# A pre-norm decoder layer: keys scaled earlier on ScalarE, scores scaled in four pieces, one residual and two transposes moved

## What is computed

```python
x = x + mixer(layernorm(x))            # in-projection, conv of 4 taps, silu, ssd, silu(z) gate, rms norm, W_out
q = rmsnorm(layernorm(x) @ Wq + bq) * qn_w
k = rmsnorm(ctx @ Wk + bk) * kn_w      # "k-hat": keys times 1/rms, per head
v = ctx @ Wv + bv
scores = q @ k.T / sqrt(128) + mask    # 1/rms of q is applied to the scores
x = x + softmax(scores) @ v @ Wo
h = silu(bit_linear(layernorm(x), w_gate)) * bit_linear(layernorm(x), w_up)
x = x + bit_linear(rms_norm(h, ln_weight), w_down)
```

## Time and profile before

| | us |
|---|---|
| median of 3 executions | 1190.26 (1189.74 to 1191.51) |
| profiled execution, device time | 1191.23 |
| its span, first to last instruction | 1189.5 |

### The profile page before, as it was taken

How to read it: one execution, slowest core, us unless ns; L and a number is a source line. 1 busy time by engine, 2 the same in 40 slices (tenths; PEclk the granted TensorE clock), 3 DMA queues, 4 the chain that set the end, 5 groups by cost and what they waited for, 6 DMA issues and landing times.

```text
span 1189.5 us, 34826 instructions
## 1 busy us (share of the span) xinstructions
PE 1119.2 (94%) x11405; PEld 983.7 (83%) x11405; DVE 1005.5 (85%) x2509; ACT 819.7 (69%) x2066; POOL 935.8 (79%) x1514
## 2 busy tenths in 40 slices
PE   4889999999999999999999999999999999999964
PEld 3678888898888889888888988888898888888753
DVE  4766898898889889888988988898898889888666
ACT  4586777677667767766776776677677667766641
POOL 4788788888888888888888888888888888878651
PEclk8899999999999999999999999999999999999987
DMA  8311101111110111111011111101111110121000
GB/s 297 87 50 24 33 17 31 37 37 35 33 37 15 29 37 37 35 33 37 15 29 37 37 35 33 37 15 29 37 37 35 33 37 15 29 35 30 22 9 23
DMA packets 103306, 46.31 MB, mean 39 GB/s; under 512 B 80352, under 2 KB 101600, under 8 KB 103008
## 3 DMA queue, kind: packets, MB, share of 16 engines
q1 hardware_dynamic: 100336, 45.75, 14.8%
q10 hardware_dynamic: 2928, 0.03, 0.1%
HBM read 23.93 MB, written 4.19 MB: 24 GB/s over the span
## 4 chain that ended last, share of the span: by engine, by line
PE 66%; DVE 13%; ACT 13%; issue 4%; POOL 2%; DMA 1%; ACTq 1%; POOLq 0%; DVEq 0%; SPq 0%
PE bank L1800 18%; PE bank L1882 5%; PE bank L1860 5%; PE bank L1718 4%; PE bank L1690 4%; PE bank L1691 4%; PE bank L1692 4%; DVE hh L1389 3%; DVE hh L1382 3%; ACT kb L875 3%; PE bank L1813 3%; PE bank L1940 2%; PE bank L1707 2%; PE bank L1870 2%; PE bank L1762 2%
## 5 line engine op out<-in xcount | busy, mean ns | idle before, releaser
L1800 PE MATMUL bank<-xcT,wq 128*128 128x128 f32 x2048 | 234.1, 275 | 2.2 <-ACT xcT L862 2.2
L1800 PEld LDWEIGHTS bank<-xcT,wq 128*128 128x128 f32 x2048 | 231.2, 192 | 2.9 <-issue 2.5
L1223 DVE SCALAR_TENSOR_TENSOR xc<-bank,cw,xc 128x124 f32<-128x124 f32 (+2 forms) x576 | 163.7, 339 | 11.6 <-ACT xc L831 3.0
L1690 PE MATMUL bank<-wo_hi,o_hi 128*128 128x256 f32 x512 | 149.5, 292 | 1.1 <-DVE o_lo L1312 1.1
L1691 PE MATMUL bank<-wo_lo,o_hi 128*128 128x256 f32 x512 | 143.7, 281 | 0.0
L1692 PE MATMUL bank<-wo_hi,o_lo 128*128 128x256 f32 x512 | 143.3, 280 | 0.0
L887 ACT ACTIVATE qT<-bank,bqT 128x128 f32<-128x128 f32 x384 | 109.6, 372 | 41.0 <-PE bank L1800 41.0
L530 POOL TENSOR_TENSOR pr<-pr,mask 128x512 f32<-128x512 f32 x64 | 79.9, 1270 | 38.1 <-DVE pr L1331 38.0
L1690 PEld LDWEIGHTS bank<-wo_hi,o_hi 128*128 128x128 f32 x512 | 96.4, 188 | 1.5 <-DVE o_lo L1312 1.4
L1691 PEld LDWEIGHTS bank<-wo_lo,o_hi 128*128 128x128 f32 x512 | 96.7, 189 | 0.1
L1692 PEld LDWEIGHTS bank<-wo_hi,o_lo 128*128 128x128 f32 x512 | 96.5, 188 | 0.0
(11 more groups left out here) (239 smaller groups left out, 3414.5 us busy)
## 6 DMA issues: line engine op xcount, KB each, us to landing
x_in<-in_x SPq DMA_DIRECT2D x32, 128.0 KB, 2.1
c_in<-in_ctx SPq DMA_DIRECT2D x32, 128.0 KB, 2.1
x_m<-in_x SPq DMA_DIRECT2D x32, 128.0 KB, 2.2
out<-x SPq DMA_DIRECT2D x32, 128.0 KB, 1.7
wq<-in_L_xattn_Wq SPq DMA_DIRECT2D x1, 2048.0 KB, 14.1
stage<-in_L_xattn_Wo SPq DMA_DIRECT2D x2, 1024.0 KB, 8.4
w_in<-in_L_attn_W_in SPq DMA_DIRECT2D x1, 1024.0 KB, 6.3
qT<-in_L_ffn_w_gate SPq DMA_DIRECT2D x1, 1024.0 KB, 12.9
```

Source lines behind the costliest of these rows:

```text
L1223: last = v.scalar_tensor_tensor(out=o, in0=src, scalar=cw[:, j, TAPS - 1 - back:TAPS - back], in1=o, op0=ALU.mult, op1=ALU.add)
L1690: mm(out, left[0], right[0], start=first, stop=False)
L1800: last = mm(x_Qbank[g][:, (n % 4) * P:(n % 4 + 1) * P], wq[:, c, n * HD:(n + 1) * HD], xcT[:, c, :], start=(c == 0), stop=(c == DC - 1))
```

## The change

Four edits. ScalarE runs `x_khat(xa)` and then `m_tanh_z(mn)` before `m_tap_bc(mn)`; they stood behind it and behind the two split copies. `x_scale` becomes two operations of 256 columns for each sequence, four in all, and the first `x_mask` waits for the third of them only. `f_residual(fb)` moves behind `m_gate(m)`. SyncE issues `turn_c` ahead of `turn_m`. TensorE's program is as before.

```diff
@@ SyncE, body(i)
                 if not isinstance(i, int) or F_TURN + 3 <= i < TILES + 1:
                     turn_f(i - 3)
+                if not isinstance(i, int) or C_TURN <= i < TILES:
+                    turn_c(i)
                 if not isinstance(i, int) or M_TURN <= i + 2 < TILES:
                     turn_m(i + 2)
-                if not isinstance(i, int) or C_TURN <= i < TILES:
-                    turn_c(i)
@@ GpSimd
             def x_mask(t, n):
-                after(pool, x_s1[1], t + 1)
+                after(pool, (x_sa, x_s1)[n][1], t + 1)
@@ ScalarE, body
                     f_keep(f)
+                if xa is not None:
+                    x_khat(xa)
                 if mn is not None:
+                    m_tanh_z(mn)
                     m_tap_bc(mn)
                 if m is not None:
                     c_split_halves(m)
                 if ms is not None:
                     m_split_halves(ms)
-                if mn is not None:
-                    m_tanh_z(mn)
-                if xa is not None:
-                    x_khat(xa)
@@ VectorE
             def x_scale(t, a):
                 after(dve, x_S[a], t + 1)
                 after(dve, s["x_rq"], t + 1)
-                v.tensor_tensor(pr[:, :, a, :], (X0, X1)[a][:, :].rearrange("p (j e) -> p j e", j=NPAIR),
-                                bcast(rq[:, 1, a * NPAIR:(a + 1) * NPAIR].unsqueeze(2), [P, NPAIR, SEQ]),
-                                ALU.mult).then_inc(x_s1[a].sem, 1)
+                for n in range(2):
+                    pairs = slice(4 * n, 4 * n + 4)
+                    v.tensor_tensor(pr[:, pairs, a, :], (X0, X1)[a][:, 256 * n:256 * n + 256].rearrange("p (j e) -> p j e", j=4),
+                                    bcast(rq[:, 1, a * NPAIR + 4 * n:a * NPAIR + 4 * n + 4].unsqueeze(2), [P, 4, SEQ]),
+                                    ALU.mult).then_inc((x_sa, x_s1)[n][a].sem, 1)
@@ VectorE, body
                     x_q_bias(xa, 1)
-                if fb is not None:
-                    f_residual(fb)
                 if ms is not None:
                     m_average(ms)
...
                 if m is not None:
                     m_skip(m)
                     m_gate(m)
+                if fb is not None:
+                    f_residual(fb)
                 if xb is not None:
                     x_o_low(xb, 0, 1)
```

More of the change, by code:

```diff
@@ L223, in decoder_layer @@
           x_chi+x_clo x_KT x_kT x_Q0+x_Q1+x_Q2+x_Q3 x_qb1 x_qb0+x_qb2+x_qb3 x_sq0+x_sq1+x_sq2+x_sq3 x_ss x_ssc x_ssT x_qv x_rq
-          x_S0+x_S1 x_scaled0+x_scaled1 x_masked0+x_masked1 x_mx0+x_mx1 x_less0+x_less1 x_ex0+x_ex1
+          x_S0+x_S1 x_part0+x_scaled0+x_part1+x_scaled1 x_masked0+x_masked1 x_mx0+x_mx1 x_less0+x_less1 x_ex0+x_ex1
           x_sum0+x_inv0+x_sum1+x_inv1 x_p0+x_p1 x_PT0+x_PT1 x_pT0+x_pT1 x_O0+x_O1
@@ L238, in decoder_layer @@
         x_q2 = [s["x_sq0"], s["x_sq1"], s["x_sq2"], s["x_sq3"]]
+        x_sa = [s["x_part0"], s["x_part1"]]
         x_S, x_s1, x_s2 = [s["x_S0"], s["x_S1"]], [s["x_scaled0"], s["x_scaled1"]], [s["x_masked0"], s["x_masked1"]]
```

## The result

The changed kernel takes 1268.0 us (median of 4, 1266.8 to 1271.4), the one before 1190.9 in the same comparison: a ratio of 1.065, interval 1.063 to 1.068. The forecast was 1270, in a range of 1232 to 1292. The profiled execution has a span of 1265.0 us.

A forecast was written before the change was run, and what follows sets the result against it. TensorE was taken to bound the kernel. From the profiled 1191.2 us, 28 x (2.12 - 0.43) = +47.3 us gave 1238.5, and +32 us for the clock gave 1270.5, predicted as 1270, range 1232 to 1292.

The forecast's parts named there:

- What bounds: Loop tile: TensorE busy 34.19 of 34.70 us sets the end; its recurring wait is for the keys' scaling, 0.43 us.
- Keys: ScalarE scales keys earlier, ending near 622.7; TensorE's 0.43 us wait goes, 28 x 0.43 = 12.0 us less.
- Context's turn: SP's queue, turn_c ahead of turn_m: nothing, bounds 0 to 0.1 us on ScalarE, none on TensorE.
- Scores: VectorE's four scaling operations take 1.5 to 1.9 us, 0.1 to 0.5 more; no gain or loss on TensorE.
- Residual: Late residual delays the store, then turn_f behind it on SP; TensorE waits 2.12 us at line 1918, 28 times.
- Clock: The stall drops TensorE's clock from 2.4 to 1.2 GHz in 20 tiles, 1.6 us each: +32 us.
- likeliest case: Stall at the feed-forward's first product plus clock falls: 1270 us, own range 1254 to 1292, chance 0.60.
- The page's rule: Trainium skill: a DMA wait per tile can lower TensorE's clock, but from a longer gap; by it the clock holds, 1238.5 us.
- the faster case: Turned activations reach TensorE in time after all, leaving only the keys' 12.0 us gain: 1179 us, chance 0.06.
- the unchanged case: Key wait reappears behind another operation and the store is not in the way: 1190 within 2 us, chance 0.03.
- the case of a stall with the clock up: TensorE stalls before the feed-forward product but its clock stays up: 1238.5 us, bounds 1232 to 1252, chance 0.29.

The follow-up runs named there:

- residual only: The kernel before with only the residual moved behind the gate product: 1270.0 us, ratio 1.067.
- stall filled, eight matmuls: The changed kernel plus eight unused 128 x 256 float32 matmuls on TensorE just before its wait at the feed-forward's first product, in 28 tiles: 1276.3 us.
- stall filled, four matmuls: The changed kernel plus four unused 128 x 256 float32 matmuls on TensorE just before its wait at the feed-forward's first product: 1238.4 us, ratio 1.040.
- residual before the gate: The changed kernel with the residual between the skip and the gate product: 1206.1 us, ratio 1.014.
- more work: The changed kernel plus two unused 128 x 256 float32 matmuls right behind f_down, in the 28 tiles of the stall: 1296.3 us, ratio 1.088.
- `turn_f` first: The changed kernel with SyncE issuing turn_f(i-3) ahead of store(i-4), residual still behind the gate product: 1175.4 us, ratio 0.986.
- context first: The kernel before with turn_c issued ahead of turn_m and nothing else: 1191.1 us, ratio 0.9998.

## Why the prediction was right

One sum holds within 3 us for the kernels with the residual behind the skip or the gate. The time is that of the kernel before (1190.9 us for the first three rows, 1190.6 for the others), plus 28 times the tile without a fall less 34.70 us, plus 1.5 us for each fall. Tile and falls are those of the one profiled execution, the measured time is the median of four:

| kernel | tile without a fall | falls | sum | measured |
|---|---|---|---|---|
| changed | 36.42 | 19 | 1267.6 | 1268.0 |
| residual only | 36.99 | 10 | 1270.0 | 1270.0 |
| stall filled, eight matmuls | 37.65 | 0 | 1273.5 | 1276.3 |
| stall filled, four matmuls | 36.43 | 0 | 1239.0 | 1238.4 |
| residual before the gate | 35.18 | 0 | 1204.0 | 1206.1 |
| more work | 38.04 | 8 | 1296.1 | 1296.3 |

- **What bounds.** TensorE, and the keys as its one wait of the loop: right. Taking the wait away leaves a tile that is 34.05 of 34.13 us matmuls.
- **Keys.** Right in kind, the term was undersized: 0.57 us a tile and not 0.43, so 15 to 17 us in all and not 12. The scaling ended at 361.94 in the tile above, 1.6 us ahead of the turning at 363.51, as forecast (though the forecast's own numbers add up to an end at 622.6, not 622.7).

```profile
360.66 1.28 ACT L876 ACTIVATE kb<-kb,kss 128x128 f32<-128x128 f32 x4
...
363.51 0.60 PE L1850 MATMUL bank<-ident,kb 128*128 128x128 f32 x4
```

- **Context's turn.** Nothing: right.
- **Scores.** Nothing on TensorE: right. The four operations take 1.44 us together, under the 1.5 to 1.9 I allowed; the first maximum waits 0.38 us for its mask and not 0.71.

```profile
668.72 1.44 DVE L1333 TENSOR_TENSOR pr<-bank,rq 128x256 f32<-128x256 f32 x4
669.91 2.50 POOL L531 TENSOR_TENSOR pr<-pr,mask 128x512 f32<-128x512 f32 x2 [0.53 <-DVE pr L1333]
671.21 0.69 DVE L1339 TENSOR_REDUCE mx<-pr 128x8 f32<-128x512 f32 x1 [0.38 <-POOL pr L531]
```

- **Residual.** The mechanism and its place were right; the run with `turn_f` first shows it. The wait was a little undersized: 2.12 us forecast, 2.23 in the records, and 36.42 - 34.13 = 2.29 in the tile. From mixer product to residual's start it took 2.94 us and not 2.83, SP's gap 0.39 and not 0.33, which is the 0.17 that was lacking. (The upper bound of 2.6 adds up to 2.5 from its own terms; both hold the wait.) As the keys gave 0.14 us more than I had put down, the two errors nearly cancelled: 36.42 us a tile without a fall, against 34.70 + 1.69 = 36.39.
- **Clock.** The step that made 28.5 of the 77 us, and the one least founded: 20 falls of 1.6 us forecast, 19 of 1.5 found. That it would fall was argued from one row of 1.80 us idle, and that the clock fell there was a matter of the execution, not of the idle time alone. The same idle stretch, 1.8 to 1.9 us before the mixer product near 55 us, stands in all 14 traces of this case. The clock fell behind it in six (before, changed, `turn_f` first, context first, four matmuls, more work) and stayed at 1.00 in the other eight. One of each, in programs that don't differ up to there, are the kernel before and the run with the residual alone:

```profile
55.00 0.69 PE L1762 MATMUL bank<-mw,xdt 64*64 64x64 f32 x32 [1.80 <-DVE xdt L1263]
...
56.00:59.40 3.40, 2.72 (x31) 1.33 (x29) 2.38 (x6) 1.15 (x4) 3.23 (x6) 1.00 0.00 0
```

  The row of 2.13 us idle proves nothing against a fall either: TensorE worked for 0.73 us behind it and stood idle for 3.86 us more, and in those the clock went to 0.50 (from 21.9 us on). The count of 20 was a value picked between 14 and 28, and that it came out was luck: the same stall in a tile 0.57 us longer gives 10. With 10 falls the changed kernel would have come out at 1254, the lower edge of the likeliest case.
- **The page's rule.** The Trainium skill ("TensorE: Matmul & The Clock Gate", "HAM oscillation — how this bites in real kernels") describes just this, a DMA wait in each tile that lowers the clock each time, but from a longer gap on. By its gap the time would have been 1238.5. The measurement decides: with stalls of 2.2 us the clock falls in 19 tiles of 28.

The rivals: the faster case is out, the unchanged case is out, and the case of a stall with the clock up is the run with the filled stall, 1238.5 us forecast and 1238.4 measured, though two terms that were too small, by 0.17 us for the stall and 0.14 for the keys, nearly cancelled in it.

## What to carry to other kernels

Before moving an operation, ask which DMA issue waits for it and what stands behind that issue in the same queue: here a store that nobody is in a hurry for held a transpose that the bound engine needs, and changing the order of the two removes the whole loss. When a stall of the bound engine comes back in each tile, price it twice, once as idle time and once at half clock behind it; here 2.3 us of the chain cost 1.0 us more a tile in the mean (19 x 1.5 / 28). And the edits off the bound engine's path (scores in four, one turn before another) were worth nothing, though the scores' own timeline got shorter. Before a cost rests on a single row, look for the same place in other traces of the same program: here the row of 1.80 us idle gave a fall in six executions of 14.

## What the runs showed of the hardware

- Idle stretches of TensorE of 1.0 us in each tile left the granted clock at 1.00; those of 2.1 to 2.3 us brought it to 0.50 in some tiles and not in others, for 3.4 us each time, and a single one of 1.8 us did so in six executions of 14. I had not expected the share to change so much with the tile's length: 19 falls of 28 at 36.42 us, 10 at 36.99, 8 at 38.04, with stalls of 2.2, 2.2 and 2.15 us. So the length of the idle stretch doesn't settle it alone. Between the 19 falls of the changed kernel lie 37.5 or 75.1 us and nothing else: three tiles with a fall, then one without. What decides it is left open.
- A small semaphore wait costs TensorE more than the idle time in its record: 0.57 us for an idle stretch of 0.43. The weight loads stand idle for 0.6 us at the same place; whether that is the reason was not tested.
- TensorE with useless matmuls in its stall made the kernel 30 us faster than with nothing in it.
